# First of the rotation's four products issued ahead of the first low probabilities on VectorE, in the attention units

## The reference

```python
a = x @ W.T + (x @ lora_A[label]) @ lora_B.T * 0.5         # a LoRA picked per batch item
q, k, v = split(a @ w_qkv.T + b_qkv)                        # 32 query heads, 8 key/value heads, 32 wide
q, k = rope(q), rope(k)                                     # out_r = xr*cos - xi*sin; out_i = xr*sin + xi*cos
p = softmax(mask(q @ k.T / sqrt(32)))                       # causal, 64 x 64 per head
x = x + (p @ v) @ w_o.T + b_o
x = x + ffn(cond2(x))                                       # two more linear maps with gated low-rank experts
```

## Time and profile before

| | us |
|---|---|
| median of 3 runs | 1148.61 |
| lowest and highest | 1147.75, 1149.65 |
| the profiled execution's own time | 1150.56 |
| its span (first to last instruction) | 1148.3 |
| TensorE busy | 1118.9 (97% of the span) |
| VectorE busy | 687.0 (60%) |
| ScalarE busy | 423.6 (37%) |
| GpSimd busy | 164.6 (14%) |

### The profile page before, as it was taken

How to read it: one execution, slowest core, us unless ns; L and a number is a source line. 1 busy time by engine, 2 the same in 40 slices (tenths; PEclk the granted TensorE clock), 3 DMA queues, 4 the chain that set the end, 5 groups by cost and what they waited for, 6 DMA issues and landing times.

```text
span 1148.3 us, 16846 instructions
## 1 busy us (share of the span) xinstructions
PE 1118.9 (97%) x6048; PEld 975.7 (85%) x6048; DVE 687.0 (60%) x1233; ACT 423.6 (37%) x1204; POOL 164.6 (14%) x130
## 2 busy tenths in 40 slices
PE   7999999999999999999979999999999999999998
PEld 6888888888888888888878998888888888888887
DVE  5312138888888888888884235233146766666664
ACT  5312125556565566555555224111122322222221
POOL 0000112333333333333241001000000000000000
PEclk9999999999999999999999999999999999999999
DMA  8020032222222332232335116383562323332122
GB/s 290 11 71 19 10 107 80 65 64 64 64 64 64 73 72 65 66 90 55 92 114 129 57 37 193 102 236 101 140 183 60 106 111 110 110 110 96 74 70 92
DMA packets 92899, 106.69 MB, mean 93 GB/s; under 512 B 8498, under 2 KB 74930, under 8 KB 92850
## 3 DMA queue, kind: packets, MB, share of 16 engines
q1 hardware_dynamic: 90146, 97.38, 28.1%
q0 software_dynamic: 2560, 8.39, 4.4%
q10 hardware_dynamic: 144, 0.26, 0.1%
HBM read 72.45 MB, written 25.17 MB: 85 GB/s over the span
## 4 chain that ended last, share of the span: by engine, by line
PE 68%; DVE 18%; ACT 8%; issue 3%; DMA 2%; POOL 0%; DVEq 0%; SPq 0%
PE psum L1583 15%; PE psum L280 13%; PE psum L1891 12%; PE psum L1314 8%; PE psum L933 6%; ACT prob L628 5%; PE psum L1969 4%; PE psum L1871 3%; DVE roped L760 2%; DVE rot_t L760 2%; PE psum L966 2%; DVE pt_l L765 2%; DVE ssum L780 2%; DVE prob L859 2%; DVE smax L857 2%
## 5 line engine op out<-in xcount | busy, mean ns | idle before, releaser
L933 PE MATMUL psum<-p_h,c_high_low 128*128 128x512 f32 (+1 forms) x768 | 195.6, 361 | 0.5 <-POOL end_l L712 0.5
L933 PEld LDWEIGHTS psum<-p_h,c_high_low 128*128 128x128 f32 x768 | 132.3, 189 | 14.3 <-issue 0.7
L280 PE MATMUL psum<-c_high_low,w_h 128*128 128x512 f32 x384 | 120.0, 398 | 5.8 <-ACT c_high_low L215 5.8
L1583 PE MATMUL psum<-ring,rows 128*128 128x512 f32 x528 | 123.7, 392 | 1.3 <-DVE t_plain L1288 1.3
L1583 PEld LDWEIGHTS psum<-ring,rows 128*128 128x128 f32 x528 | 98.8, 188 | 24.2 <-DVE t_plain L1288 2.6
L1314 PE MATMUL psum<-chunk,rows 128*128 128x384 f32 (+1 forms) x576 | 108.6, 343 | 4.2 <-DVE rows L1182 2.5
L1314 PEld LDWEIGHTS psum<-chunk,rows 128*128 128x128 f32 x576 | 101.8, 190 | 5.4 <-issue 3.2
L933 PE MATMUL psum<-p_l,c_high_low 128*128 128x512 f32 (+1 forms) x384 | 103.0, 363 | 0.0
L280 PEld LDWEIGHTS psum<-c_high_low,w_h 128*128 128x128 f32 x384 | 73.8, 192 | 22.6 <-ACT c_high_low L215 5.8
L708 POOL TENSOR_TENSOR c_high_low<-ring_plain,c_high_low 128x512 fp32r<-128x512 f32 x32 | 41.3, 1291 | 329.8 <-ACT c_high_low L589 190.1
L628 ACT ACTIVATE prob<-prob 128x64 f32<-128x64 f32 x240 | 58.1, 244 | 54.1 <-DVE prob L859 54.1
(11 more groups left out here) (172 smaller groups left out, 2174.9 us busy)
## 6 DMA issues: line engine op xcount, KB each, us to landing
ring_plain<-in_x_t SPq DMA_DIRECT2D x32, 256.0 KB, 3.0
ring_plain<-attn_scratch SPq DMA_DIRECT2D x32, 256.0 KB, 4.0
raw<-x_t_scratch SPq DMA_DIRECT2D x16, 512.0 KB, 4.2
rest<-in_b_base SPq DMA_DIRECT2D x16, 512.0 KB, 4.4
out<-rest SPq DMA_DIRECT2D x15, 512.0 KB, 2.9
ring_plain<-in_wqkv_t SPq DMA_DIRECT2D x10, 512.0 KB, 6.1
a_raw<-in_lora_a SPq DMA_DIRECT2D x32, 128.0 KB, 2.1
ring_plain<-ring_plain POOLq DMA_DIRECT2D x16, 256.0 KB, 3.5
```

Source lines behind the costliest of these rows:

```text
L280: mm = pe.matmul(to, stationary, moving, start=k == 0 and m == 0, stop=k == KT - 1 and last, skip_group_check=True)
L933: mm = pe.matmul(to, sx[:, kk, :], moving(w, n, kk), start=first, stop=False, skip_group_check=True)
L1583: mm = pe.matmul(self.psum[:, self.BANK_OF[i], :], w[:, cols], s, start=m == 0 and p == 0, stop=m == KT - 1 and p == 2, skip_group_check=True)
```

## The change

The rotation's code is split in two functions. `first_product` holds the four waits and issues the first of the four products; `rotate` issues the other three, the subtraction and the addition. In the steps that have both "score" and "main" (steps 1 to 15), `first_product` now stands at the start of the step, ahead of the first `pt_l`. In step 1 nothing stands between the two, and in step 16 the order is as it was, so the order of instructions differs in the 14 steps 2 to 15.

```diff
-        def rotate(v, part):
-
+        def products(part):
             pairs = qkv[:, 0:QK].rearrange("p (h i two) -> p h i two", i=HD // 2, two=2)
             for n, (dst, table) in enumerate(((roped[:, :, :, part], (cos, sin)[part]), (rot_t[:, part, :, :], (sin, cos)[part]))):
-                last = dve.tensor_tensor(dst, pairs[:, :, :, n], table[:, :].unsqueeze(1).to_broadcast([P, NH, HD // 2]), ALU.mult)
-            last.then_inc((rot_re, rot_im)[part], 1)
+                yield dve.tensor_tensor(dst, pairs[:, :, :, n], table[:, :].unsqueeze(1).to_broadcast([P, NH, HD // 2]), ALU.mult)
+
+        def first_product(v):
+            dve.wait_ge(qkv_out, v + 1)
+            dve.wait_ge(const_in, 16 * len(consts))
+            need(dve, rotated, 2 * v)
+            need(dve, qk_t, 3 * v)
+            real = products(0)
+            next(real)
+            return real
...
         def step(u, main, score, value, nxt):
             v, w = u - 1, u - 2
+            if score and main:
+                real = first_product(v)
             if value:
...
             if score:
...
+                if not main:
+                    real = first_product(v)
+                rotate(v, real)
```

More of the change, by code:

```diff
@@ L755, in vector, with rotate @@
     def vector(dve):
-        def rotate(v, part):
+        def products(part):
             pairs = qkv[:, 0:QK].rearrange("p (h i two) -> p h i two", i=HD // 2, two=2)
             for n, (dst, table) in enumerate(((roped[:, :, :, part], (cos, sin)[part]), (rot_t[:, part, :, :], (sin, cos)[part]))):
-                last = dve.tensor_tensor(dst, pairs[:, :, :, n], table[:, :].unsqueeze(1).to_broadcast([P, NH, HD // 2]), ALU.mult)
-            last.then_inc((rot_re, rot_im)[part], 1)
+                yield dve.tensor_tensor(dst, pairs[:, :, :, n], table[:, :].unsqueeze(1).to_broadcast([P, NH, HD // 2]), ALU.mult)
[7 more added lines that the diff above has]
+            return real
+        def rotate(v, real):
+            next(real).then_inc(rot_re, 1)
+            *_, last = products(1)
+            last.then_inc(rot_im, 1)
+            dve.wait_ge(rot_re, v + 1)
+            dve.tensor_tensor(roped[:, :, :, 0], roped[:, :, :, 0], rot_t[:, 0, :, :], ALU.subtract).then_inc(rotated, 1)
+            dve.wait_ge(rot_im, v + 1)
+            dve.tensor_tensor(roped[:, :, :, 1], roped[:, :, :, 1], rot_t[:, 1, :, :], ALU.add).then_inc(rotated, 1)
         def probs_low(w, b):
```

## The result

The changed kernel takes 1164.17 us (median of 4 runs, 1163.32 to 1166.54); on the same chip the kernel before took 1148.28. The ratio is 1.0138, with a 95% interval of 1.0125 to 1.0152: 1.4% slower, 15.9 us. Predicted were 1164.2 us. In the ratios of this document two single runs far outside all others of their kernel are left out, one of 1374 us (e1_before_short) and one of 3200 us (the kernel before, beside e3 to e6).

The account below looks back on a forecast made before the run. A step is set by the later of VectorE's and TensorE's rows at L952, the transposes of q and k. 14 steps x 1.12 = 15.7 us on 1148.61 gives 1164.3, forecast as 1164.2 us; range 1159.5 to 1168.

Parts of the forecast that it names:

- The hole: VectorE between the third bias addition and the first pt_l: 0.51 us idle, 14 times; the product starts there near 330.26.
- The hold: The early product, with two SBUF inputs, stands until GpSimd's L718 ends at 331.70, and ends at 332.38; chance 0.86.
- L1182's two rows: VectorE's L1182, 1.22 us alone, took 1.89 and 3.43 beside GpSimd work, ending 1.08 and 1.07 us after it.
- room of 0.55 at L952: TensorE's transposes of rotated q and k could start at 336.91 but start at 337.46, waiting for VectorE's second pt_l.
- A: Rival: the product beside L718 is not held, L952 comes 0.18 us earlier a step: 1146.1 us; chance 0.08.
- B: Rival: product and L718 go at half speed while they overlap, L952 0.64 late: +9.0, 1157.6 us; chance 0.03.
- C: Rival: TensorE's new stop in attend halves its clock, up to 1.7 us a step on top: 1188 us; chance 0.03.
- TensorE's side: Projection matmuls up to L952 1.67 us late; less the room of 0.55, L952 is 1.12 late a step.
- VectorE's side: Second product, rotation and second pt_l 1.02 us late; by this side L952 would be 1.02 late.

Follow-up runs that it names:

- e1_before_short: Kernel before, with GpSimd's second normalising of a step (L718) cut from 128x1024 to 128x16x2 elements: 1148.24 us, ratio 0.9995.
- e3: Changed kernel with GpSimd's last two pieces of a step exchanged, L718 ahead of L708: 1148.34 us, 0.9996 of the kernel before.
- e6: Changed kernel with GpSimd's second normalising (L718) waiting until the early product is done: 1156.24 us, 1.0063 of the kernel before.
- e1: Changed kernel with GpSimd's second normalising (L718) cut to 128x16x2 elements: 1145.21 us, 0.9969 of the kernel before.
- e7_pool_order_waits: Changed kernel with GpSimd's L718 ahead of L708 and the product's wait for qkv_out placed last: 1146.75 us, 0.9986 of the kernel before.
- e4: Changed kernel with attend and the second transposes 1.5 us later in TensorE's row: 1162.83 us, 1.0126 of the kernel before.

## Why the prediction was right

1. *The hole.* The product was expected 0.23 us after the last bias addition, and started 0.22 after it. With the wait for `qkv_out` last it is 0.1.
2. *The hold.* Expected: the product ends 0.68 behind L718, so takes 2.12. Measured: 2.14, 0.68 to 0.69 behind in all 14 steps. The figure came from L1182's two rows, of other tensors, another width, and without a repeated input; it held for this product with its table of 16 numbers. e1 shows that L718 is the cause, e6 that the hold goes with the instruction that meets L718, and e3 that whichever comes first keeps going, in both directions.
3. *pt_l.* Expected 2.26 us after the bias addition, measured 2.28; its own duration (1.21) was as expected. In this kernel it runs behind L718 and not beside it; that it isn't slowed beside it is seen in the earlier trace rows and in e6 (1.22).
4. *TensorE.* A new stop, forecast as 1.67 by starts and some 1.7 in the profile; the profile gives 1.48 for matmuls and 1.69 for loads. Its room of 0.55 at L952 was used up, so the wait there went away from the list. Forecast 1.12 a step, measured 1.13 in the step shown (27.89 - 26.76) and 1.11 on average (15.5 over 14).
5. *VectorE.* Forecast 1.02 late. e4 gives the step of that side alone: 27.77 - 26.76 = 1.01.
6. *Every step.* All 14 had it. Its sum was forecast as 15.7 us; the attention stage grew by 15.5.
7. *Rivals.* A (no hold) is refuted by the product's 2.14 us, but its sum was right: with the hold gone e1 has the step 0.18 shorter, and 0.31% were measured, 3.5 us and not 2.5. The remaining 1 us isn't explained; it is within the interval (0.9957 to 0.9980 is 2.3 to 4.9 us). B (sharing) is refuted by L718's 1.90 us, unchanged. C (the clock) by the granted 1.00.

What was right by luck is the last digit: the prediction started from a median of 1148.61 and added 15.7, the result is 1148.28 and 15.9, and the median of the runs before moved by 0.4 us from one comparison to the next. TensorE's side and VectorE's side were only 0.1 us apart, so the size of the step would have come out nearly the same had the wrong one been taken; e4 shows that the right one was.

## What to carry to other kernels

Before moving a VectorE instruction into a gap, look at what GpSimd does in that gap, and count the moved instruction's inputs in SBUF: with two of them it doesn't finish before a GpSimd elementwise instruction with inputs in SBUF that is under way has ended (here it ended 0.68 us later), and all that is queued behind it is late too. A gap of 0.5 us beside such a GpSimd instruction is worth nothing to it; a reduction with one input in SBUF used the gap and cost only what stood out of it (0.82 us of work, 0.42 a step), and `pt_l`, with an input in PSUM, ran there at its normal length. Where both must run, what counts is the end of GpSimd's instruction, so move that one, and see that VectorE's is in the queue before GpSimd's next one.

## What the runs showed of the hardware that was not expected

- The tail is very constant: the held product ended 0.68 us behind the GpSimd instruction in all 14 steps of the changed kernel, in e3 and in e6, whether it had stood for 0.1 us or for 1.5 us. It is the instruction's time alone (0.82 to 0.83) less 0.14.
- A GpSimd instruction is held the same way: L708 took 1.88 us in place of 1.30 behind a product that was in the queue 0.16 us before it, and ended 1.15 behind the product (225.44 and 224.29 in the second step of e3): again its time alone less some 0.14. VectorE's waiting product got in ahead of GpSimd's next instruction, although GpSimd went from one to the next without a pause.
- The order of waits matters on VectorE. With the binding wait (the one that ends last) ahead of the register steps the product started 0.22 us after the last bias addition, with the binding wait last 0.10. In the one step outside the loop, where the waits read no register, it is the other way round: 0.03 with the binding wait first (changed kernel), 0.13 with it last (e7_pool_order_waits), from the starts of the 14 products in the traces. Why, no run shows.
